# Graph units: the contexts of two key steps in one run behind every fourth score round, with sixteen entries in the ring of exponentials

## The reference

```python
x = x + _L0_attn_ref(_layernorm(x), mask, W_qk, W_v, W_out, b_out, conv)
x = x + _L0_ffn_ref(_layernorm(x), ew, act_w, We, be, Wq, Wk, Wv, Wo, ln_g, ln_b)
```

```python
def _mha(q, k, v, wq, wk, wv, wo):
    qh, kh, vh = ((a @ w).reshape(B, S, H, dh) for a, w in ((q, wq), (k, wk), (v, wv)))
    scores = jnp.einsum('bqhd,bkhd->bhqk', qh, kh) / jnp.sqrt(dh)
    attn = jax.nn.softmax(scores, axis=-1)
    return jnp.einsum('bhqk,bkhd->bqhd', attn, vh).reshape(B, S, d) @ wo

for c in range(6):                       # nodes; q, k, v come from earlier nodes
    q = ew[c, 0] * (nodes[in_q] @ We[eq] + be[eq])   # k and v alike
    nodes[c] = act_w[c] * _mha(q, k, v, Wq[c], Wk[c], Wv[c], Wo[c]) + q
```

## Time and profile before

| what | value |
|---|---|
| median of 3 runs (lowest, highest) | 3216.39 us (3213.2, 3227.56) |
| the profiled execution's own time | 3224.36 us |
| its span | 3222.5 us |
| busy: TensorE, its weight loads, VectorE, ScalarE, GpSimd | 91%, 41%, 75%, 67%, 12% of the span |
| exponentials of the graph (L1569) | 1516 of 1.025 us |
| maxima of the graph (L1594), two products / one | 1.207 us / 0.685 us |
| contexts of the graph (L1475) | 6144 instructions |

### The profile page before, as it was taken

How to read it: one execution, slowest core, us unless ns; L and a number is a source line. 1 busy time by engine, 2 the same in 40 slices (tenths; PEclk the granted TensorE clock), 3 DMA queues, 4 the chain that set the end, 5 groups by cost and what they waited for, 6 DMA issues and landing times. The chain is left out here.

```text
span 3222.5 us, 49154 instructions
## 1 busy us (share of the span) xinstructions
PE 2925.9 (91%) x19007; PEld 1308.3 (41%) x19007; DVE 2415.2 (75%) x3075; ACT 2145.9 (67%) x2683; POOL 380.4 (12%) x322
## 2 busy tenths in 40 slices
PE   5698998989869999999999999999999999999994
PEld 4365555555433333333333333333333333333331
DVE  5654555556578888888888888888888888888843
ACT  1154555545427777777777777777777777777783
POOL 0000000000001111111111111011111111111114
PEclk9699999999969999999999999999999999999996
DMA  6000000001342534443444354434534443444302
GB/s 175 17 11 1 27 2 11 18 20 43 71 81 61 111 96 104 86 96 94 95 95 106 94 109 73 102 95 87 109 94 108 77 101 94 89 105 101 59 22 87
DMA packets 144399, 243.90 MB, mean 76 GB/s; under 512 B 56562, under 2 KB 92934, under 8 KB 140838
## 3 DMA queue, kind: packets, MB, share of 16 engines
q1 hardware_dynamic: 143590, 238.67, 33.2%
q10 hardware_dynamic: 576, 2.10, 0.2%
HBM read 163.82 MB, written 74.10 MB: 74 GB/s over the span
## 5 line engine op out<-in xcount | busy, mean ns | idle before, releaser
L1569 ACT ACTIVATE pt_b<-ps_max 128x1024 f32<-128x1024 f32 x1516 | 1492.0, 1025 | 366.3 <-PE ps_max L1440 360.0
L1594 DVE TENSOR_REDUCE mx_b<-ps_pair 128x2 f32<-128x1024 f32 (+1 forms) x989 | 1193.7, 1207 | 164.1 <-PE ps_pair L1426 155.0
L1475 PE MATMUL ps_ctx<-pt_b,vs 128*32 128x512 f32 x6144 | 818.9, 605 | 3.8 <-ACT c_b L1558 3.5
L1594 DVE TENSOR_REDUCE mx_b<-ps_misc 128x1 f32<-128x512 f32 x989 | 677.9, 685 | 147.5 <-PE ps_misc L1426 128.4
L1440 PE MATMUL ps_max<-qs,ks 50*128 50x512 f32 x3032 | 781.5, 436 | 4.7 <-PEq L549 4.1
L1426 PE MATMUL ps_pair<-ks,qs 48*128 48x512 f32 x1955 | 511.8, 457 | 84.2 <-DVE mx_b L1594 84.2
L1440 PEld LDWEIGHTS ps_max<-qs,ks 50*128 50x128 f32 x3032 | 352.9, 185 | 343.8 <-ACT pt_b L1569 250.5
L1426 PE MATMUL ps_misc<-ks,qs 48*128 48x512 f32 x989 | 441.6, 447 | 7.2 <-DVE mx_b L1594 0.3
L930 ACT ACTIVATE pt<-ps_max,cb 128x512 f32<-128x512 f32 x338 | 213.5, 685 | 256.8 <-PE ps_max L776 200.7
L1426 PEld LDWEIGHTS ps_pair<-ks,qs 48*128 48x128 f32 x1955 | 207.7, 184 | 363.8 <-DVE mx_b L1594 333.7
L1426 PEld LDWEIGHTS ps_misc<-ks,qs 48*128 48x128 f32 x989 | 182.9, 185 | 333.9 <-DVE mx_b L1594 254.4
(11 more groups left out here) (194 smaller groups left out, 2296.3 us busy)
## 6 DMA issues: line engine op xcount, KB each, us to landing
partd<-part SPq DMA_DIRECT2D x22, 2048.0 KB, 9.4
qs<-partd SPq DMA_DIRECT2D x288, 128.0 KB, 5.7
ks<-partd SPq DMA_DIRECT2D x288, 128.0 KB, 6.7
xv<-node SPq DMA_DIRECT2D x24, 512.0 KB, 5.5
xf<-node SPq DMA_DIRECT2D x24, 512.0 KB, 4.7
node<-nt_b SPq DMA_DIRECT2D x48, 256.0 KB, 2.1
rec_b<-invd SPq DMA_DIRECT2D x368, 32.0 KB, 1.8
xq<-node SPq DMA_DIRECT2D x22, 512.0 KB, 3.7
```

The lines of the kernel that those rows point to most:

```text
L1475: ins = pe.matmul(psO[SLOT * i:SLOT * i + SLOT, :], vs[u % 2][:, kb, QUAD * (s // HALF_STEPS) + i], pt[:, (QUAD * S + i) % ENTRIES], start ...
L1569: act.activation(pt[:, e:e + 2].rearrange("p k n -> p (k n)"), at[:], ACT.Exp, scale=SCALE_B).then_inc(exp_done, 1)
L1594: nc.vector.tensor_reduce(mx2[:, at:at + n], (psP, psX)[p % 2][:, 0:CHUNK * n].rearrange("p (h n) -> p h n", h=n), AX.X, ALU.max).then_inc ...
```

## The change

Two numbers and one range. `ENTRIES` goes from 12 to 16, so that the ring of exponentials holds four steps in place of three. `steps_at` now gives its steps out in pairs (`TOGETHER` = 2): the contexts of an even step are no longer issued behind the second round after its last score, but together with those of the odd step after it, two rounds later.

```diff
@@ -46,7 +46,8 @@
 NE = 512
 HALF_STEPS = NCHUNK * KB
 PIECES = QUAD * KB
-ENTRIES = 3 * QUAD
+TOGETHER = 2
+ENTRIES = (TOGETHER + 2) * QUAD
 
 NODES = 6
 UNITS = NODES * BATCH
@@ -1262,7 +1263,7 @@
         def steps_at(u, r):
 
             since, until = (max(filled(u, k) - LAG[u == LAST], NS * u - LAG[0]) for k in (r, r + 1))
-            return range(max(0, since // QUAD), max(0, until // QUAD))
+            return range(*(TOGETHER * max(0, k // (QUAD * TOGETHER)) for k in (since, until)))
 
         GROUP_ROUND = {BASE[u] + r: (S + 1) // KB - 1 for u in range(UNITS) for r in range(len(ROUND[u]))
                        for S in steps_at(u, r) if S % KB == KB - 1}
```

## The result

The changed kernel takes 3661.56 us (median of 4 runs, 3634.76 to 3669.15) against 3217.62 us before: 1.136 times the time, 95% interval 1.130 to 1.142. The forecast was 3461 with a range of 3380 to 3505. The direction was right; the loss is 444 us, where 245 had been worked out.

A forecast was written before the change was run, and what follows sets the result against it. TensorE was taken as the only engine near full in the graph. Waits of 10.5 us a unit on 23 units (241) plus 4 in the last gave 245: profiled 3224.4 to 3469, median 3216.4 to 3461, range 3380 to 3505.

The forecast's parts named there:

- Four S between two runs of C: Four score rounds between runs of contexts: two score tiles make TensorE wait; loss 10.5 us a unit.
- the eight plain blocks: Blocks of four score rounds without other rounds, in a middle unit: 43.9 us against 38.3 before, loss 5.6.
- The eight others: Blocks with other rounds, in a middle unit: 59.7 us against 54.8 before, loss 4.9.
- Sixteen runs of C a unit in place of 32: Fewer, longer runs of contexts on TensorE: 3.8 us a unit saved if TensorE were never kept waiting.
- The larger ring: Four more entries for exponentials: no exponential waits for the ring in either order, nothing gained or lost.
- The last unit: Last graph unit, bounded by ScalarE, with three tiles: 4 us more, bounds 0 and 8.
- The played 3.97: Last unit, four score rounds with one run of two steps' contexts, worked out: 3.97 us.
- The base of 3.79: Last unit before the change: 3.79 us for four rounds, from context bank copies 15.17 apart over eight steps.
- Together 10.5 a unit, on 23 units 241 us: Losses of plain and other blocks summed over the units before the last; with 4 for the last, 245 us.
- The larger loss: Rival: late engines carry delay into the next block, 0.11 us more each, 12.3 a unit; 3507 us, chance 0.08.
- C C: TensorE's run of contexts for two steps together, closing each block of four score rounds: 1.86 us.
- the block played: Plain block shown by the change, worked out event by event: 5.19 us against about 4.31 before.

The follow-up runs named there:

- e_ring: The larger ring of sixteen entries alone, contexts of one step as in the kernel before: 3218.54 us, ratio 0.9993 to the kernel before.
- e_pairs12: The runs of two steps alone, against the kernel before, with its ring of twelve entries: 3672.82 us, ratio 1.140.
- e_pairs_last: The kernel before with runs of two steps in the last unit alone: 3221.4 us, ratio 1.0016.
- e_refill: The changed kernel with scores of every second and third round of a four-round block written twice (second and third in the last unit): 3510.17 us, ratio 1.0895.
- e_phase: The kernel before with the pieces of the maxima given out half a piece earlier: 3272.17 us, ratio 1.018.

## Why the prediction was right in direction and wrong in size

*"Four S between two runs of C: the loss."* Right, event by event, in the blocks at full clock. Its size, 10.5 us a unit, is 10.3 in them. Of the two parts, the eight plain blocks make 43.8 us (43.9 played). The eight others make 59.6 (59.7 played); that this sum came so near is partly luck, for four of them took 0.1 us more than played, and the one with the second values round 0.5 less. What the prediction says in words, that the third and fourth S wait for exponentials, is half of it: ahead of the fourth stands a wait for a reduction.

*"Sixteen runs of C a unit in place of 32: a gain."* Right: a run of two takes 1.86, and the gain appears, 67 us, once nobody waits.

*"The larger ring: nothing gained, nothing lost."* Right (e_ring, e_pairs12).

*"The last unit: 4 us, bounds 0 and 8."* At full clock 2.6 (e_pairs_last), in the changed kernel 5.4: within the bounds both times. The played 3.97 for four rounds is met. The base of 3.79 was taken from two copies of the bank and holds a share of a copy; without it four rounds took 3.62. That the sum is near all the same is luck: in the stretch around the output round the changed order is 0.9 us quicker, which was not played.

*"Together 10.5 a unit, on 23 units 241 us. Sum: 245."* This is the step that failed, by what it left out. Every rate of TensorE in the sum was read at full clock, and the sum kept it there while it put waits into every block (in the first block shown above TensorE is empty for 0.7 of 5.17 us). The missing term is what the low clock costs: 112.2 - 103.4 = 8.8 us in a middle unit. The whole account, from the profiled executions:

| part | forecast, us | shown, us |
|---|---|---|
| ahead of the graph | 0 | -13 |
| 23 units, waits at full clock | 241 | 23 x 10.3 = 237 |
| 23 units, clock | nothing | 446.8 - 237 = 210 |
| last unit | 4 | 5.4, of it 2.8 in rounds at low clock |
| sum | 245 | 439 |

The medians differ by 444. That the 10.3 of the middle units hold in the first and the last of the 23 as well is assumed.

*The larger loss, 0.08, to 3507.* It looked for more of the same mechanism, with engines that start late; at full clock the sixteen blocks add up to the unit as played. What happened is in none of the listed cases: no rival has a lower clock.

It could have been seen. The attention ahead of the graph, in the kernel before:

```profile
250.00:970.00 720.00, 635.61 (x5016) 388.54 (x5012) 412.39 (x515) 356.42 (x543) 30.16 (x25) 0.92 0.13 31
```

TensorE was busy there for 635.6 of 720 us, 88%, and was granted 0.92. A unit of the graph was at 96% and 1.00. The forecast unit had the same work in 103.6 us, that is about 86%: nearer to the attention's row than to the graph's, and so the clock of the graph's row could not be taken for granted. A unit of the changed kernel came out at 89% and 0.91. The share is a warning and no more, for it does not order the rows by itself. A unit of e_refill was busy for 93% and stood at 1.00, a unit of e_phase for 95% and stood at 0.95, and a slow product counts as busy for longer.

What the clock would cost can be estimated from rows of the kernel before. At the attention's 0.92 the unit of 103.6 us becomes at most 103.6 / 0.92 = 112.6 us, if TensorE's work fills all of the slow time; measured are 112.2. After the fact the price can be read from either level: C C takes 1.86 us or 3.44. The 427 us at the lower level in 21 units cost 21 x 8.8 = 185 us, 0.43 us for each, where 0.5 would be the price if TensorE had worked throughout.

## What to carry to other kernels

Fewer, longer runs on the bounding engine save their entries only if the buffers between it and its readers hold a whole run's worth of work. Here two score tiles hold at most 1.9 us of exponentials, just what C C takes, and in the block played 1.2 us of it were left when C C began (3.33 to 4.53); and the pieces in between must wait for their own reader. Play one cycle by hand, with start, length and release of each engine from the timeline: in this case it gave the length of fifteen of sixteen kinds of block at full clock within 0.13 us.

When such a cycle puts waits into TensorE's time, the waits may not be the whole price. Say at which clock the durations of the sum were read. Look in the same profile for stretches in which TensorE has as much idle time as it will have after the change, and if their rows show a lower granted clock, work out the sum at that clock as well, as a rival with a chance of its own.

Short of removing waits, harmless repeated products in them can be the cheaper evil: e_refill got back 151 of 444 us, and still lost to the kernel before. It is a test for the cause of a low clock before it is a remedy.

## What was not expected of the hardware

The granted clock fell although no single wait of TensorE in the middle units was long: in the units 1 to 21 it is never empty for more than 0.9 us at a time. The rows of waits above (total us, times, longest) have 0.9 us as TensorE's longest wait for a reduction or for an exponential. The kernel before, whose clock stayed up, has the same longest wait, but fewer of them, 140 instead of 385:

```profile
PE ps_pair L1426 <- DVE mx_b L1594: 84.2, 140, 0.9
```

And the low clock shows mostly in runs of C C, where TensorE works without a gap: 72% of the time at the lower level lies in them, and they are 34% of the graph's time. The run at 2042.68 was at full clock, the one at 2047.86 was not, with waits of 0.46 and 0.24 us between them. What exactly the chip weighs is left open; no run here was made to find it.

A second surprise is the neighbourhood: the order of the kernel before, disturbed only in where the pieces stand (e_phase), lost the clock in some units and kept it in others of the same order, with units of 94.0 and 99.1 us.
